# Opening the token phase's first block inside attention's last units

## The reference

```python
h = _layernorm(x) * (1 + ca) + sa
x = x + ga * _L0_attn_ref(h, qkv, wo)      # softmax(q k^T / 4, causal) v, then @ wo.T
h = _layernorm(x) * (1 + cb) + sb          # first thing after attention, token by token
x = x + gb * _L0_ffn_ref(h, W_r, W_k, W_v, mu_r, mu_k)
# where, in _L0_ffn_ref, x_prev is the token before:
k = (mu_k * x + (1.0 - mu_k) * x_prev) @ W_k.T
r = sigmoid((mu_r * x + (1.0 - mu_r) * x_prev) @ W_r.T)
out = r * (square(relu(k)) @ W_v.T)
```

## Time and profile before

| | |
|---|---|
| median of 3 runs | 2154.98 us (2153.86 to 2155.17) |
| the profiled execution | 2159.02 us, of which the span is 2157.3 us |
| mean granted TensorE clock in it | 0.978 of full |
| attention, from the page's lines and the trace | 144 to 1351.4 us |
| token phase from its first PE instruction | 1355.03 us to the end |
| busy in the span | PE 90%, DVE 79%, ACT 66%, POOL 43% |

### The profile page before, as it was taken

How to read it: one execution, slowest core, us unless ns; L and a number is a source line. 1 busy time by engine, 2 the same in 40 slices (tenths; PEclk the granted TensorE clock), 3 DMA queues, 4 the chain that set the end, 5 groups by cost and what they waited for, 6 DMA issues and landing times. The chain is left out here.

```text
span 2157.3 us, 30286 instructions
## 1 busy us (share of the span) xinstructions
PE 1944.2 (90%) x10299; PEld 838.3 (39%) x10427; DVE 1704.2 (79%) x2499; ACT 1423.1 (66%) x1921; POOL 928.2 (43%) x823
## 2 busy tenths in 40 slices
PE   7889999988999989999899998699999977999997
PEld 4442222222222222212222222566665544777775
DVE  6779999999999999999999999367888774333332
ACT  5768999988999989999889998345445421111110
POOL 5764454433334433443433344234555552433434
PEclk9999999999999999999999999799999988999999
DMA  6652220122212021217220100201010013544541
GB/s 207 200 166 45 43 34 9 25 47 45 32 23 32 23 47 23 33 22 230 74 58 13 35 3 20 65 20 40 31 40 30 26 58 105 120 107 97 121 105 24
DMA packets 123390, 133.73 MB, mean 62 GB/s; under 512 B 33753, under 2 KB 117554, under 8 KB 122544
## 3 DMA queue, kind: packets, MB, share of 16 engines
q1 hardware_dynamic: 108656, 117.86, 20.4%
q0 software_dynamic: 14592, 14.08, 3.7%
HBM read 96.85 MB, written 50.63 MB: 68 GB/s over the span
## 5 line engine op out<-in xcount | busy, mean ns | idle before, releaser
L1270 DVE SCALAR_TENSOR_TENSOR arena<-ps_s,arena 128x1024 f32<-128x1024 f32 (+1 forms) x1071 | 1146.9, 1139 | 41.4 <-ACT arena L1233 33.3
L1233 ACT ACTIVATE arena<-ps_s 128x1024 f32<-128x1024 f32 (+1 forms) x1194 | 1040.8, 934 | 109.4 <-PE ps_s L1176 96.1
L1176 PE MATMUL ps_s<-arena 128*128 128x512 bf16 (+3 forms) x2176 | 580.5, 365 | 104.3 <-DVE arena L1270 77.9
L1192 PE MATMUL ps_o<-arena,values 128*32 128x512 f32 (+3 forms) x4608 | 565.7, 568 | 9.1 <-ACT arena L1222 4.3
L1282 POOL TENSOR_SCALAR arena<-arena 128x512 f32<-128x512 f32 x123 | 236.4, 1922 | 499.7 <-ACT arena L1238 499.4
L1176 PEld LDWEIGHTS ps_s<-arena 128*128 128x128 bf16 x2304 | 154.9, 97 | 694.4 <-DVE arena L1270 532.6
L1849 ACT ACTIVATE arena<-t_ps_four 128x320 f32<-128x320 f32 (+1 forms) x96 | 42.0, 438 | 298.6 <-PE t_ps_four L1724 298.6
L2185 POOL DMA_INDIRECT out<-values,slot_ids x80 | 123.6, 1545 | 221.1 <-DVE values L2101 194.3
L1724 PE MATMUL t_ps_four<-arena 128*128 128x320 f32 (+1 forms) x768 | 214.0, 435 | 0.6 <-DVE arena L2060 0.6
L1192 PEld LDWEIGHTS ps_o<-arena,values 128*32 128x32 f32 x4608 | 94.0, 108 | 233.1 <-issue 185.4
L2073 DVE TENSOR_TENSOR arena<-t_ps_four,arena 128x320 f32<-128x320 f32 (+1 forms) x96 | 47.2, 492 | 166.3 <-ACT arena L1849 166.3
(11 more groups left out here) (201 smaller groups left out, 1713.5 us busy)
## 6 DMA issues: line engine op xcount, KB each, us to landing
arena<-parts_dram SPq DMA_DIRECT2D x320, 64.0 KB, 2.2
parts_dram<-arena SPq DMA_DIRECT2D x32, 384.0 KB, 2.9
arena<-parts_dram SPq DMA_DIRECT2D x24, 512.0 KB, 7.1
slots_in_dram<-in_empty_slots SPq DMA_DIRECT2D x10, 1040.0 KB, 25.4
arena<-slots_in_dram SPq DMA_DIRECT2D x16, 650.0 KB
arena<-in_L_ffn_w_gate SPq DMA_DIRECT2D x16, 352.0 KB
arena<-in_L_ffn_w_up SPq DMA_DIRECT2D x16, 352.0 KB
arena<-in_L_attn_x SPq DMA_DIRECT2D x8, 512.0 KB, 4.2
```

Source lines behind the costliest of these rows:

```text
L1176: last = pe.matmul(ps_s[:, unit.bank + i, p.at:p.at + p.width], m.k_stack[:, group.g % 2 * HG + p.head, p.kt * P:p.kt * P + P], q_stack[:, ...
L1192: last = pe.matmul(ps_o[32 * p.head:32 * p.head + 32, p.w0:p.w0 + p.width], m.values_flat[:, at:at + 32], probs[:, job.at % PROB_BANKS, p. ...
L1233: act.activation(probs[:, unit.slot:unit.slot + n], ps_s[:, unit.bank:unit.bank + n], ACT.Exp, scale=1.0 / DH ** 0.5).then_inc(exped, 1)
L1270: dve.scalar_tensor_tensor(p, ps_s[:, unit.bank:unit.bank + n], 0.0, p, ALU.not_equal, ALU.mult).then_inc(bank, 1)
```

## The change

Token block 0's turn, copy, output projection, sum, statistics and norm leave the token phase and are done in attention. Two units without jobs are put into the plan, each holding a pair of score banks: `open_turn`, when 24 jobs or fewer are left, and `open_out`, when 5 or fewer are left. PE turns block 0's rows in the first and projects them in the second; ACT copies the turned rows right at `open_turn`; POOL scales w_o there (one instruction for what DVE did in two). DVE adds x and takes the statistics after the last mask; POOL's deviation and ACT's norm stand at the end of their programs for attention. In the token phase block 0's stages of these names return at once, and DVE does `other_weights` not at the beginning but after `constants`, in step 2 of `staged`. The other branch (scores too large) gets the same steps at its end. Semaphores and the buffers for these results are placed ahead of the phases.

```diff
+    a = Carver(m.arena2, 2 * TT * D)
+    m.ln_c = Norm(m, ctx, "t_ln_c", a)
+    m.opened_at = a.at
+    a.take(KC, BT)
+    m.attnT_first = a.take(KC, BT)
+    m.xn_first = a.take(TT, D)
...
+def open_turn(m, pe, ps):
+
+    pe.wait_ge(m.attn_in[0], 16)
+    for k in range(KC):
+        for t in range(TT):
+            last = pe.transpose(ps[:, k, t * P:t * P + P], m.attn_rows[:, 0, t, k * P:k * P + P], m.ident[:])
+        last.then_inc(m.turned[k], 1)
...
+def open_out(m, pe, ps):
+
+    pe.wait_ge(m.turn_taken[1], 1)
+    pe.wait_ge(m.w_o_scaled, 1)
+    for c in range(2):
+        for t in range(2):
+            at = (2 * c + t) * P
+            for k in range(KC):
+                last = pe.matmul(ps[:, c, t * D:t * D + D], m.attnT_first[:, k, at:at + P], m.w_o[:, k], start=k == 0, stop=k == KC - 1)
+        last.then_inc(m.out_made[c], 1)
...
+def open_take(m, act, ps, widened):
+
+    act.wait_ge(widened, 5)
+    for k in range(KC):
+        act.wait_ge(m.turned[k], 1)
+        act.activation(m.attnT_first[:, k], ps[:, k], ACT.Copy).then_inc(m.turn_taken[k], 1)
...
+def open_add(m, dve, ps):
+
+    dve.wait_ge(m.x_again[0], 16)
+    for c in range(2):
+        dve.wait_ge(m.out_made[c], 1)
+        x = m.x[:, 2 * c:2 * c + 2]
+        dve.tensor_tensor(x, ps[:, c].rearrange("p (t n) -> p t n", t=2), x, ALU.add).then_inc(m.out_taken[c], 1)
+    for c in range(2):
+        dve.wait_ge(m.out_taken[c], 1)
+    m.ln_c.statistics(dve, 0, m.x[:, 0:TT])
...
+def open_scale(m, pool, widened):
+
+    pool.wait_ge(widened, 5)
+    pool.wait_ge(m.weights_in, m.weights_expected)
+    pool.tensor_tensor(m.w_o, m.w_o, m.gates[:, 0, 0:1].to_broadcast([P, KC, D]), ALU.mult).then_inc(m.w_o_scaled, 1)
+    pool.memset(m.mhalf[:], -0.5).then_inc(m.half_set, 1)
...
+LEFT_AT = {"open_turn": 24, "open_out": 5}
...
+        openings = ["open_turn", "open_out"]
         while taken < len(jobs) or turned < BLOCKS:
             left = len(jobs) - taken
             if n % 4 < 3:
-                if left:
+                if openings and left <= LEFT_AT[openings[0]]:
+                    self.units.append(Unit(n, at, openings.pop(0), []))
+                elif left:
                     self.units.append(Unit(n, at, "pair" if left > 1 else "single", jobs[taken:taken + 2]))
                     taken += len(self.units[-1].jobs)
                 at += 2
...
-            scored += unit.kind != "turn"
+            scored += len(unit.jobs) > 0
```

```diff
@@ -1206,6 +1308,12 @@
                 for unit in plan.units:
                     if unit.kind == "turn":
                         turn_over(unit)
+                    elif unit.kind == "open_turn":
+                        wait_bank(unit)
+                        open_turn(m, pe, ps_s[:, unit.bank:unit.bank + 2])
+                    elif unit.kind == "open_out":
+                        wait_bank(unit)
+                        open_out(m, pe, ps_s[:, unit.bank:unit.bank + 2])
                     else:
                         score(unit)
                     for group in plan.weighed_after[unit.n]:
...
-                    if unit.kind != "turn":
+                    if unit.kind == "open_turn":
+                        open_take(m, act, ps_s[:, unit.bank:unit.bank + 2], widened)
+                    if unit.jobs:
...
                         copy_out(b)
+                open_norm(m, act)
             with act.If(flag < 1):
                 other[2](act)
...
+                    elif unit.kind == "open_out":
+                        opened = ps_s[:, unit.bank:unit.bank + 2]
+                    elif unit.kind in ("pair", "single"):
                         n = len(unit.jobs)
                         dve.wait_ge(exped, unit.scored + 1)
 
                         p = probs[:, unit.slot:unit.slot + n]
                         dve.scalar_tensor_tensor(p, ps_s[:, unit.bank:unit.bank + n], 0.0, p, ALU.not_equal, ALU.mult).then_inc(bank, 1)
+                    if unit is plan.final:
+                        open_add(m, dve, opened)
...
+                    if unit.kind == "open_turn":
+                        open_scale(m, pool, widened)
...
+                open_deviation(m, pool)
             with pool.If(flag < 1):
                 other[4](pool)
...
             def turn_attn(b):
+                if b == 0:
+                    return
                 pe.wait_ge(m.attn_in[b % 2], 16 * (b // 2 + 1))
                 turn("attn", b, attn[:, b % 2])
 
             def attend_out(b):
+                if b == 0:
+                    return
                 pe.wait_ge(turn_taken[1], turns.through("attn", b))
-                if b == 0:
-                    pe.wait_ge(weighted, 1)
                 rows_out("attend", b, attnT, m.w_o)
 
             def turn_attended(b):
                 pe.wait_ge(ln_c.normed, b + 1)
-                turn("attended", b, xn_c)
+                turn("attended", b, xn_c if b else m.xn_first)
...
             def take_attn(b):
-                if b:
+                if b == 0:
+                    return
+                if b > 1:
                     act.wait_ge(out_made[1], outs.through("attend", b - 1))
...
             def add_attended(b):
+                if b == 0:
+                    return
                 dve.wait_ge(m.x_again[b], 16)
                 for c in range(2):
                     dve.wait_ge(out_made[c], outs.through("attend", b))
@@ -1887,8 +2013,6 @@
                 for c in range(2):
                     dve.wait_ge(out_taken[c], outs.through("attend", b))
                 ln_c.statistics(dve, b, x_of(b))
-                if b == 0:
-                    other_weights()
...
             dve.wait_ge(m.weights_in, m.weights_expected)
-            for k in range(KC):
-                last = dve.tensor_tensor(m.w_o[:, k], m.w_o[:, k], m.gates[:, 0, 0], ALU.mult)
-            last.then_inc(weighted, 1)
             for k in range(KC):
...
                 then(dve.tensor_copy(m.h_wide[:, :, D], token))
+                other_weights()
 
             staged([(4, residual), (6, add_shared), (2, mix), (2, mix_again), (1, add_attended), (4, add_delta),
```

More of the change, by code:

```diff
@@ L815, in number_units @@
         for unit in self.units:
-            banks = range(unit.bank, unit.bank + max(len(unit.jobs), 1))
+            banks = range(unit.bank, unit.bank + (2 if unit.kind in LEFT_AT else max(len(unit.jobs), 1)))
             self_before = [holder[b] for b in banks if b in holder]
@@ L831, in place_weighing @@
     def place_weighing(self):
+        self.final = [unit for unit in self.units if unit.jobs][-1]
         self.weighed_after = {unit.n: [] for unit in self.units}
@@ L947, in sync @@
             load_x_again(m, sp, b)
+        sp.sem_inc(reloaded, 1)
     def gpsimd(pool):
@@ L995, in tensor @@
         units(pe, unit, finish=finish)
+        pe.wait_ge(reloaded, 1)
+        open_turn(m, pe, ps_first)
+        open_out(m, pe, ps_second)
     def scalar(act):
@@ L1155, in wait_bank @@
                         pe.wait_ge(o_ready, other.turned + 1)
+                    elif other.kind == "open_turn":
+                        for k in range(KC):
+                            pe.wait_ge(m.turn_taken[k], 1)
+                    elif other.kind == "open_out":
+                        for c in range(2):
+                            pe.wait_ge(m.out_taken[c], 1)
                     elif other.kind == "shared":
```

50 lines of the change are left out of this document (36 added, 14 removed).

## The result

| | before | after |
|---|---|---|
| median of 10 runs each, us | 2155.21 (2153.85 to 2159.10) | 2147.05 (2143.75 to 2151.18) |
| ratio, 95% interval | 1 | 0.9963 (0.9953 to 0.9973) |
| profiled span, us | 2157.3 | 2144.9 |

The account below looks back on a forecast made before the run. Attention was taken as paced by DVE, with PE and ACT nearly full, and block 0 as running alone at the token phase's start. 5.0 us added less 13.95 removed gives -8.95: 2154.98 becomes 2146.0, range 2142.0 to 2152.0.

Parts of the forecast that it names:

- The removed part: Token phase, from PE's first instruction to `mix_keys`: 8.9 us where it was 22.84, so 13.95 us less.
- X: PE's first instruction of the token phase; predicted to come 5.0 us later, together with attention's end.
- `open_turn`, 1.8: In attention, block 0's turn and copies: DVE waits 0.7 us, PE's late weighing adds 1.1, together 1.8.
- `open_out`, 2.4: Near attention's end, PE's projection: 5.35 us until the next mask against 2.9 of DVE masks, so DVE stands 2.4.
- C: Rival: both openings stall at their upper bounds; with B's 2.65 a gain of 2.3 us is left, 2152.7; chance 0.13.
- A: Rival: DVE's masks in attention hide both openings at 0 us; gain 13.15, 2141.8; chance 0.12.
- The tail, 0.8: After attention's last mask: the last store is issued 4.65 us after it instead of 3.84, 0.8 more.
- `other_weights`, 0: Token phase: DVE's 4.5 us fits its 5.33 idle before block 0's product with the gate, 0.5 spare; cost 0.
- The block's end: End of attention: SP drains 7.75 us after the last mask, ACT ends at 7.7; nothing added beyond 0.8.
- B: Rival: ACT ends the block, paying SP's 2.7 us: +2.65, gain 6.3, 2148.7; chance 0.24, shared with larger stalls.
- Sum: Whole kernel: 1.8 + 2.4 + 0.8 = 5.0 us added, 13.95 removed; everything from `mix_keys` on moves by -8.95.
- D: Rival: PE's clock stays at half beyond X + 6.5 in the token phase: +5.35 us, 2160.3, slower; chance 0.03.

Follow-up runs that it names:

- change_again: The changed kernel run once more, unaltered: 2147.25 us, ratio 0.9952.
- weights_later: The kernel before with only DVE's other_weights moved, to after the constants of step 2: 2155.6 us, ratio 1.0.
- turn_only: The change with only block 0's turn, copy and w_o scaling in attention; projection, sum, statistics and norm back in the token phase: 2154.49 us, ratio 0.9996.
- projection_twice: The change with block 0's projection issued twice on PE into the same banks: 2147.11 us, ratio 0.9962.
- projection_split: The change with block 0's projection in two halves on PE, the second after the square group's weighing: 2145.37 us, ratio 0.9946.

## Why the prediction was right, and where it was not

**The removed part.** Predicted 13.95, measured 14.69 and 14.42. The mechanism stood: the prediction gave two ways to `mix_keys`, PE's projection (X + 8.8, with half clock until X + 6.5) and the path over ACT, POOL and DVE (X + 8.2). Which of them ended last was left to the clock. In the first trace it was at 1.00 from X + 3.6, PE was done at X + 7.3, and the other path set `mix_keys`, 8.15. In change_again it was at 0.50 until X + 6.3, almost the assumed 6.5, and PE set it, 8.42. The start value varies with the clock too: the 22.84 before was 23.61 in weights_later. PE has no pause between its turns and the projection in either trace of the change, so the pause of 0.69 that the kernel before has there does not explain the difference. Why the clock rose sooner in one execution no run isolates.

**`open_turn`, 1.8.** turn_only measures 1.47. **`open_out`, 2.4.** 2.59 are left to it (16.46 less 13.87), as a wait of 2.50. Together 4.06 for 4.2. projection_twice and projection_split show the reasoning. The prediction set DVE's 2.9 us of masks against the lump plus 1.73 (scores, exponential, waits) that must follow it before the next mask, so 1.17 of the lump should be covered. Lumps of 1.95, 3.68 and 7.13 left waits of 0.78, 2.50 and 5.96, each its length less 1.17 or 1.18. C and A fall.

**The tail, 0.8.** 0.88, of which turn_only, with no addition, has 0.86: in both PE's last weighing waits for the triangle's cuts and starts 1.0 after the last mask, where before it started 0.15 after it. DVE's additions are covered.

**`other_weights`, 0.** Right in sum, but the spare of 0.5 was not there:

```profile
1377.88 0.43 DVE L2003 TENSOR_TENSOR arena<-arena,mod_rows 128x256 f32<-128x256 f32 x1
...
1378.32 0.69 DVE L2037 TENSOR_TENSOR arena<-t_ps_out,arena 128x512 f32<-128x512 f32 x1
```

It ends at 1378.31, and the product with the gate follows without a wait where there were 5.33. One more of these instructions ahead of it would have cost.

**The block's end.** This is the step that failed: "So nothing is added beyond 0.8, if ACT again drains at once". ACT did drain at once, and B with its 2.65 falls. Yet X came 1.05 to 1.15 late: SP drained 4.2 and 4.1 after the store's issue instead of 3.1 (in change_again PE came last, at 4.3), where the prediction had counted its time from issue to drain as fixed (0.4 + 2.7). In both traces of the change a second 16 KB fetch falls beside the last store, and the store lands late. When ACT jumps elsewhere, one 16 KB fetch there, the late landing and the 1.1 us go together (one execution). That the fetch was ACT's, and that it held up the store and the other engines' fetches, is my reading and not shown; nor is whether X waits for the store or for a fetch that is late like it. ACT's place alone does not make it: in projection_twice, with the same norm, ACT reaches its drain 1.0 after the store's issue as in the change, yet there are two fetches in that 1.1 us and no delay. Only PE's program differs there.

**Sum.** At `mix_keys` -8.70 and -8.34 for -8.95: 0.7 and 0.5 too little taken out, 0.1 too much put in, 1.1 at the block's end missed. Two misses of opposite sign nearly cancel, and that the sum came within 0.3 to 0.6 is in part luck. D falls: no stretch at 0.50 reaches `mix_keys`.

## What to carry to other kernels

A chain that runs alone at the start of a phase can be worth moving into the phase before even where that is full. Here a lump on an engine beside the pacing one cost its length less a fixed cover, and the cover was smaller than the pacing engine's backlog, since the work between the lump and the pacing engine's next instruction came off it: 2.9 us of backlog covered 1.2 here. Split in two, with the second half where PE had time, 3.7 us cost 0.8 instead of 2.5. Split in two a few units earlier they cost more than in one piece, mainly because PE had to wait for the opening's banks. Work put between the masks costs its own time on DVE.

At the end of a block ask of each engine when it jumps and what its fetch falls beside; a jump can be put where the engine waits anyway. Effects of 1 to 3 us in a program of 2150 are measured from a common instruction ahead of the change, since one stretch of 416 us varies by 5 with the granted clock.

## What the runs showed of the hardware

- With the jumps over the untaken branch at attention's end, four to seven instruction fetches are made between the last store and X (three with ACT's jump elsewhere in the change), and SP, PE and DVE need 2.5 to 5.1 us from last instruction to drain. ACT pays nothing that shows: its drain begins 1.6 us before its norm ends. Made by all engines at attention's start, the jumps cost 3.8 us there, with five fetches.
- Two fetches of 16 KB beside a store of 128 KB: it lands after 3.7 and 4.1 us. With one or none it lands after 2.0 to 2.8.
- From attention's last store to the token phase's first PE instruction pass 3.6 to 3.9 us in most traces with jumps at the end, 4.7 and 4.8 in the two traces of the change, and 3.1 with no jump in it, then set by the last engine's own work.
- TensorE's granted clock at the start of a phase differs between executions of one kernel: 0.50 until 3.6 and until 6.3 us after X. The same float32 projection takes 3.62 and 4.93 us.
- Over one stretch the mean granted clock is 0.94 to 0.96 from trace to trace, and the stretch takes 418.6 to 413.2 us.
